# Inverse blocks in four parts, key products by chunks, and two first tiles prepared a stage ahead

## The reference

```
q, k, v = [silu(causal_conv4(x @ W.T)) for W in (Wq, Wk, Wv)]
beta = sigmoid(x @ Wb.T)
q, k = l2norm(q), l2norm(k)
# per head and per chunk of 32 tokens
A = strict_lower(-(beta*k) @ k.T);  T = inverse(eye - A)
u = T @ (beta*v);  w = T @ (beta*k)
# scan over chunks with state S
u_adj = u_i - w_i @ S
o_i = q_i @ S + causal(q_i @ k_i.T) @ u_adj;  S = S + k_i.T @ u_adj
# three causal per-channel filters of v, 3, 15 and 63 taps, and a gate
probs = softmax((x @ gate_w + gate_b) / exp(log_temp)) * (1 - 5*eps) + eps
o = p0*fir_s(v) + p1*fir_m(v) + p2*fir_l(v) + p3*delta + p4*v
attn = rmsnorm(o) @ Wo.T
x1 = layernorm(x + attn);  out = layernorm(x1 + ffn(x1))
```

## Time and profile before

| | us |
|---|---|
| median of 3 runs | 2274.93 |
| lowest, highest | 2270.86, 2278.68 |
| the profiled execution itself | 2272.73 |
| its span, first to last instruction | 2270.9 |
| TensorE busy in the span | 2067.6 (91%) |
| VectorE, ScalarE, GpSimd busy | 1163.6, 884.8, 521.0 |

### The profile page before, as it was taken

How to read it: one execution, slowest core, us unless ns; L and a number is a source line. 1 busy time by engine, 2 the same in 40 slices (tenths; PEclk the granted TensorE clock), 3 DMA queues, 4 the chain that set the end, 5 groups by cost and what they waited for, 6 DMA issues and landing times.

```text
span 2270.9 us, 41455 instructions
## 1 busy us (share of the span) xinstructions
PE 2067.6 (91%) x16936; PEld 1753.8 (77%) x16936; DVE 1163.6 (51%) x1803; ACT 884.8 (39%) x1438; POOL 521.0 (23%) x530
## 2 busy tenths in 40 slices
PE   7888882778699999599999999999999999999998
PEld 5776762667588887488888888888888888888886
DVE  5777776974377776334334434434433443443442
ACT  4455541110244444234434434434443443443442
POOL 1111777875355555100000000000000000000000
PEclk9999995798699999699999999999999999999999
DMA  5666667677999996100000000000000000000000
GB/s 166 195 195 167 209 181 195 222 220 276 211 233 236 238 236 161 60 1 28 1 28 28 1 28 28 1 28 28 6 23 28 29 1 28 28 1 28 28 1 19
DMA packets 246751, 217.02 MB, mean 96 GB/s; under 512 B 158786, under 2 KB 210498, under 8 KB 241986
## 3 DMA queue, kind: packets, MB, share of 16 engines
q1 hardware_dynamic: 234306, 184.29, 29.6%
q10 hardware_dynamic: 12288, 30.41, 4.5%
HBM read 130.52 MB, written 84.15 MB: 95 GB/s over the span
## 4 chain that ended last, share of the span: by engine, by line
PE 56%; DVE 1%; issue 1%; ACT 1%; DMA 0%; POOLq 0%; DVEq 0%; SPq 0%; POOL 0%; ACTq 0%
PE B L1534 50%; PE O L1561 5%; PE T L1492 1%; DVE yb L1667 0%; ACT gate L1606 0%; DMA srow<-in_srow 0%; DVE stats L1695 0%; DVE stats L1729 0%; ACT L1606 0%; DVE x L1690 0%; DVE z L1720 0%; DVE xl L1647 0%; DVE z L1724 0%; DVE x L1708 0%; DVE z L1743 0%
## 5 line engine op out<-in xcount | busy, mean ns | idle before, releaser
L1620 ACT ACTIVATE yb<-B,scol 128x512 f32<-128x512 f32 x256 | 176.7, 690 | 580.2 <-PE B L1534 580.2
L1534 PE MATMUL B<-act1l,wr 128*128 128x512 f32 x1024 | 398.5, 389 | 0.0
L1534 PE MATMUL B<-act0h,wr 128*128 128x512 f32 x1024 | 398.3, 389 | 0.0
L1534 PE MATMUL B<-act0l,wr 128*128 128x512 f32 x1024 | 398.3, 389 | 0.0
L1534 PE MATMUL B<-act1h,wr 128*128 128x512 f32 x1024 | 398.3, 389 | 0.0
L1655 DVE TENSOR_TENSOR act0l<-yb,act0h 128x512 fp32r<-128x512 f32 x256 | 176.2, 688 | 317.4 <-ACT act0h L1623 315.2
L453 DVE SCALAR_TENSOR_TENSOR acc<-proj,taps,acc 128x512 f32<-128x512 f32 x288 | 214.7, 750 | 84.4 <-ACT acc L399 75.8
L1655 DVE TENSOR_TENSOR act1l<-yb,act1h 128x512 fp32r<-128x512 f32 x128 | 88.6, 692 | 295.5 <-ACT act1h L1623 295.5
L1534 PEld LDWEIGHTS B<-act0l,wr 128*128 128x128 f32 x1024 | 192.2, 188 | 39.9
L1534 PEld LDWEIGHTS B<-act1l,wr 128*128 128x128 f32 x1024 | 192.2, 188 | 39.9
L1534 PEld LDWEIGHTS B<-act1h,wr 128*128 128x128 f32 x1024 | 192.2, 188 | 39.9
(11 more groups left out here) (169 smaller groups left out, 3204.0 us busy)
## 6 DMA issues: line engine op xcount, KB each, us to landing
qk_s<-yT SPq DMA_DIRECT2D x16, 1024.0 KB, 6.1
kk_s<-kfull SPq DMA_DIRECT2D x16, 1024.0 KB, 6.4
qk<-qk_s SPq DMA_DIRECT2D x32, 512.0 KB, 4.2
wraw<-in_ffn_w ACTq DMA_DIRECT2D x32, 352.0 KB, 5.0
toe<-in_toe_short ACTq DMA_DIRECT2D x32, 320.0 KB, 7.4
xt<-in_xt SPq DMA_DIRECT2D x16, 524.0 KB, 4.3
k_s<-ktok SPq DMA_DIRECT2D x16, 512.0 KB, 7.2
v_s<-vtok SPq DMA_DIRECT2D x16, 512.0 KB, 3.2
```

Of the source, the lines that this page charges most:

```text
L1534: last = nc.tensor.matmul(B[slot % 4][:, :], w, part, start=(k == 0 and i == 0), stop=(k == kts - 1 and i == len(parts) - 1))
L1620: last = nc.scalar.activation(dst, B[slot % 4][:, :], ACT.Gelu, scale=scol[:, slot:slot + 1])
```

## The change

The inverse's 8 slots are cut into four parts of 2 slots and 4 steps each. Parts 0 and 1 go to GpSimd within project, parts 2 and 3 to VectorE in weights_fir, where their 60 operations lie in groups 4 to 55 instead of 0 to 29. Key products are made per 64 tokens, all in `keys`, with 64 x 64 results; `kk_s` is half as large. The steps of project are written out without loops. Gate tables of three quarters of the rows are computed in project after steps 4, 8 and 12; weights_fir computes the last quarter. Window 0 of `win` is filled by SP from `vtok` in project, the first three Toeplitz tiles are loaded at its start. The load and norm of the first feed-forward tile stand at the end of delta. `y` has two buffers. In the diff, `gate_logits` stands for four operations of VectorE (bias, temperature, maximum, subtraction), `gate_shares` for five (sum, reciprocal, slope, scaling, eps). The pieces are, in order: constants and `blocks_in`, SP, TensorE, ScalarE and VectorE in project, VectorE in weights_fir, SP and VectorE in delta, and the size of `kk_s`.

```diff
+EARLY = 2
+EARLY_COLS = {6: (0, 1, 8), 7: (0, 8, 14), 8: (0, 14, 20), 9: (0, 20, 31),
+              10: (1, 1, 8), 11: (1, 8, 14), 12: (1, 14, 20), 13: (1, 20, 27), 14: (1, 27, 31)}
...
+        first = q // 2 * PGRP + t * NS % PGRP
+        queue.dma_start(keep["tri"][first:first + NS, c * PSLOTS + q % 2, :, :],
...
+                    sp.dma_start(win0[:, NT + t * BATCH:NT + (t + 1) * BATCH, :], vtok[p][:, 0, :, :]).then_inc(v_stored[p], 16)
+                    sp.dma_start(win0[WIN:P, t * BATCH:(t + 1) * BATCH, :], vtok[p][0:WIN, 0, :, :]).then_inc(v_stored[p], 16)
+                    if t + 1 < STEPS:
+                        sp.dma_start(win0[0:WIN, (t + 1) * BATCH:(t + 2) * BATCH, :], vtok[p][WIN:P, 0, :, :]).then_inc(v_stored[p], 16)
...
+                    for s in range(BH):
                         b, hh = s // KT, s % KT
+                        for chunk in HALVES:
+                            for par in range(2):
+                                kt = yT[p][64 * par:64 * par + DK, KT + hh, b * P + chunk.start:b * P + chunk.stop]
+                                last = nc.tensor.matmul(side[par][chunk, s * HC:s * HC + HC], kt, kt, start=True, stop=True)
+                    last.then_inc(kk_ready, 1)
...
-                after = {0: keys, 1: lambda t, p: squared(t, p, 2), 2: small, 4: values}
+                after = {0: keys, 2: small, 4: values}
...
+                for t in range(STEPS):
+                    step(t, t % 2, t // 2, t > 0)
...
+                for n in range(NTOE):
+                    toeplitz(act, io, keep, n)
+                act.wait_ge(prm_in, 16)
+                nc.scalar.activation(itemp[:, :], prm[:, NGATE:NGATE + HEADS], ACT.Exp, scale=-1.0).then_inc(itemp_done, 1)
...
+                for t in range(1, STEPS):
+                    step(t, t % 2, (t - 1) // 2, True, t < 2)
+                    if t % PART_STEPS == 0:
+                        c = t // PART_STEPS - 1
+                        act.wait_ge(small_out, t + 1)
+                        if c < EARLY:
+                            if c:
+                                act.wait_ge(gam0_done, c)
+                            nc.scalar.activation(ebeta[:, :, :], raw[:, c * NE:c * NE + NE, NGATE:NGATE + HEADS], ACT.Exp,
+                                                 scale=-1.0).then_inc(exp0_done, 1)
+                        act.wait_ge(to_exp0, c + 1)
+                        nc.scalar.activation(lg0[:, :, :, :], lg0[:, :, :, :], ACT.Exp).then_inc(exp0_done, 1)
...
+                for t in range(1, STEPS):
+                    step(t, t % 2, (t - 1) // 2, True)
+                    if t % PART_STEPS == 0:
+                        first_logits(t // PART_STEPS - 1)
+                        if t // PART_STEPS <= EARLY:
+                            first_scales(t // PART_STEPS - 1)
+                    if t % PART_STEPS == 1 and t > 1:
+                        first_shares(t // PART_STEPS - 1)
...
+def gate_logits(nc, link, keep, lg, mx, rows):
...
+def gate_shares(nc, link, keep, lg, mx, rows):
...
+        OPS = 2 * (CH - 2)
+        SUB_FIRST, SUB_END = 4, 4 + OPS * 13 // 15
+        D_OUT, T_OUT = {2: 0, 6: 1, 29: 2, 30: 3}, {4: 0, 8: 1, 30: 2, 31: 3}
+        TURNS = {2: (0,), 5: (1,), 28: (2, 3)}
...
+                    if n == 1:
+                        for c in range(EARLY, PARTS):
+                            blocks_there(dve, keep, c)
+                        dve.wait_ge(tables_out, 3)
+                        dve.wait_ge(above_zero, 1)
+                        sub.scaled_columns().then_inc(columns_scaled, 1)
+                        dve.wait_ge(columns_scaled, 1)
+                    if n == 2:
+                        query_scales()
+                    if SUB_FIRST <= n < SUB_END:
+                        for i in range((n - SUB_FIRST) * 15 // 13, (n - SUB_FIRST + 1) * 15 // 13):
+                            link(sub.update(i // 2 + 1) if i % 2 else sub.outer_product(i // 2 + 1))
+                    if n == SUB_END:
                         dve.wait_ge(upper_zero, 1)
+                        sub.scaled_rows().then_inc(keep["inv_done"][1], 1)
...
+                for p in range(2):
+                    sp.wait_ge(y_stored[p], 48)
+                sp.dma_start(keep["x1"][:, :, :], row(io["y_s"], 0)).then_inc(keep["x1_in"][0], 16)
+                sp.dma_start(keep["xres"][:, :, :], io["x"][:, 0:P, :].rearrange("b p d -> p b d")).then_inc(keep["xres_in"], 16)
...
+                nc.vector.tensor_tensor(x1[:, :, :], x1[:, :, :], xres[:, :, :], ALU.add).then_inc(keep["x1_sum"], 1)
...
-    "kk_s": (P, GRP, P),
+    "kk_s": (P, GRP, HC),
```

More of the change, by code:

```diff
@@ new lines, in toeplitz, with by_matrix @@
+def toeplitz(act, io, keep, n):
+    toe, toe_in = keep["toe"][n % NTOE], keep["toe_in"][n % NTOE]
+    act.dma_start(toe[:, NF - 1, :, :], io["toe_long"][n]).then_inc(toe_in, 16)
+    act.dma_start(toe[SHORT:, 0:NF - 1, :, :], io["toe_short"][n]).then_inc(toe_in, 16)
+def by_matrix(nc, gam, half):
+    for par in range(2):
+        last = nc.vector.tensor_copy(gam[:, :, par, :],
+                                     half.rearrange("p (v b) (k r) -> p v r (b k)", b=GB, r=2)[:, :, par, :])
+    return last
@@ L560, in weights_fir, with turn_scales @@
+def turn_scales(nc, out, gam, ident, parts=1):
+    for c in range(parts):
+        for rows in HALVES:
+            last = nc.tensor.matmul(out[rows, c * HC:c * HC + HC],
+                                    gam[rows, c * 2 * PART_STEPS:(c + 1) * 2 * PART_STEPS, :, :].rearrange("p t r s -> p (t r s)"),
+                                    ident[rows, rows], start=True, stop=True)
+    return last
 def weights_fir(nc, sems, io, keep):
@@ L726, in _, with turn @@
[L726 to L729 removed]
+                def turn(c):
+                    inverses_there(act, c)
+                    if c >= 2:
+                        act.wait_ge(turned_stored[c % 2], 64 * (c // 2))
+                    nc.scalar.activation(turned_inv[c % 2][:, :, :, :],
+                                         tri[:, c * PSLOTS:c * PSLOTS + PSLOTS, :, :].rearrange("p q i c -> p q c i"),
+                                         ACT.Copy).then_inc(turned, 1)
@@ L744, in _ @@
                 for n in range(HEADS * DK // TCH - NTOE):
                     act.wait_ge(conv_ready, (n + 1) * PER_TOE)
-                    toeplitz(n + NTOE)
-                    if n in TURNS:
-                        turn(TURNS[n])
+                    toeplitz(act, io, keep, n + NTOE)
+                    for c in TURNS.get(n, ()):
+                        turn(c)
             @block.vector
@@ L1382, in ffn @@
         ln_eps = outer.sb("ln_eps5", [P, BATCH])
-        x1 = [outer.sb(f"x1{i}", [P, BATCH, D]) for i in range(2)]
+        x1 = [keep["x1"], outer.sb("x11", [P, BATCH, D])]
         z = [outer.sb(f"z{i}", [P, BATCH, D]) for i in range(2)]
```

459 lines of the change are left out of this document (221 added, 238 removed).

## The result

The changed kernel took 2243.6 us (median of 4 runs, 2240.09 to 2253.28) against 2276.8 (4 runs on the same chip): a ratio of 0.9868, interval 0.9839 to 0.9897. It is about 30 us (1.3%) faster, where 47 to 49 were forecast. The time lies in the range 2207 to 2247, 18 us above the point, and outside the 2215 to 2238 that the forecast claimed for itself. The profiled execution took 2240.09 us with a span of 2238.3, 32.6 less than before.

The account below looks back on a forecast made before the run. Bounds: a TensorE-ScalarE-VectorE ring in projections, VectorE then TensorE in the filter loop, TensorE in the feed-forward. Projections -4, filter stage -34.6, entry -8.7: -47.3 us, forecast 2226 (chance 0.50), own range 2215 to 2238, wide range 2207 to 2247.

Parts of the forecast that it names:

- Gate tables and scales three times inside: Projections: three places of gate and scale work cost 12 us against 5 for one before: +7 us (0 to +15).
- The filter stage: Second stage, weights_fir: preamble -24.9, loop -12.7 and its end +3 us, together -34.6 us.
- Rival A: Filter loop: transfers set its time, 196 us at 226 GB/s; stage gains 21 us, not 34.6; 2240 in all; chance 0.15.
- C: Filter preamble goes only in part, tables still wait for slow clock or a transfer: 16 us more, 2242; chance 0.08.
- Key products by chunks: Projection steps: TensorE's 1.33 us wait goes, 0.65 us a step gained: -9.8 us (0 to -20); last step -2.8.
- the ends of the loops' 0.3: Projections: unrolling saves the odd 0.3 us at each loop turn, six iterations: -1.7 us (0 to -12).
- Start, stage end, ninth step, preamble: Projections: start +3 us, end -1.5, GpSimd overrun in the ninth step +1.5; filter preamble, first weighting at 9 us: -24.9.
- The loop: Filter and inverse loop: 151 us plus 10 for transfers and low clock, 161 against 173.7: -12.7 us (-22 to -4).
- the charge of GpSimd: Filter loop: GpSimd's operations delay VectorE's inverse work by 0.42 us in each of 52 groups.
- the reading that the prediction set aside: Filter loop: the 0.42 us paid per pair of operations, 30 times as before; the loop would be 9 us less.
- below 5 us: Filter loop: sign that TensorE's waits for toe, the filter tiles, stay under this total.
- Stage end and entry of the feed-forward: Filter stage's end: late block stores, +3 us (0 to +8); feed-forward entry without the tile's loads: -8.7 us (-7 to -9.5).

Follow-up runs that it names:

- e_warm2: Changed kernel plus unread TensorE matmuls in the two steps behind each gate place, cut to the gap (7 and 3, then 6): 2231.9 us, ratio 0.9812.
- e_warm: Changed kernel plus unread TensorE matmuls in the two steps behind each gate place (12 and 5, then 11): 2239.0 us, ratio 0.9833.
- e_dense: Changed kernel with VectorE's inverse operations at the old density, two a group in groups 4 to 33: 2255.4 us, ratio 0.9909.
- e_place: Changed kernel with gate and scale pieces behind steps' last filters and exponentials in ScalarE's gap before a step's last SiLU: 2234.6 us, ratio 0.9825.

## Why the prediction was right in direction and too large

**The step that failed** is the term "Gate tables and scales three times inside": 12 us for three places against 5 for the one before, +7. The places cost 31.7 us, less 1.1 that the step after the second regains: about +26. (GpSimd was 1.1 us late to one square; TensorE's steps show the same sum.) The price of the work itself was set somewhat low: at a clock of 1.00 it is 3.6 us at the first place (e_warm2; forecast 2.7), at most 7.8 at the second (e_warm; 5.2), 6.2 at the third (e_warm2). The prediction had 4.2 for that one. Together at most 17.6 for 12, so of the 19 us that the term is off, at most 6 are the work and the rest, 13 or more, is a term that the prediction did not have: TensorE's lower clock behind its wait. It is 6.8 of 10.4 us at the first place and 3.4 of 9.6 at the third. The prediction read the clock in the loop and never in the projections. The hint was there: the earlier trace rows gave one place at 23.31, and it was taken as the price of the work, while the clock was down in that very step of the kernel before:

```profile
215.00:220.00 5.00, 3.71 (x21) 3.08 (x22) 2.25 (x3) 3.21 (x7) 0.00 (x0) 0.66 1.01 230
```

**The total is nearer than its parts.** The filter stage won 39.2 us where 34.6 were forecast, which covers a quarter of the miss in the projections. 2243.6 lies where rivals A (2240) and C (2242) stood, and neither happened: the preamble went whole, and the filter stage gained more and not less. That the time is inside the wide range is in part luck.

**Key products by chunks.** Quiet steps of 19.6 us: met, with the ends of the loops' 0.3. The step had a second effect, not forecast: two waits of TensorE became one of 1.7 us. That this made the falls of the clock likelier is argued, not shown.

**Start, stage end, ninth step, preamble.** First xt at 13.2 us and not 9.1; the stage's last stretch 27.8 us (31.0 before); GpSimd had no gap in front of the square after step 9 and was 1.1 us late to it, which VectorE did not feel (1.5 us were booked for it); first weighting 9.4 us into the stage (9 forecast). All met within 1.5 us, though 1.9 of the 24.9 us forecast for the preamble were a wait of the second weighting, which stands in the loop of the table (it took 1.92 us).

**The loop.** -17.5 where -12.7 was forecast. Too high was the charge of GpSimd: the groups on VectorE are now

```profile
L155 DVE TENSOR_TENSOR outer<-tri 128x120 f32<-128x120 f32 (+14 forms) x30 | 32.6, 1086 | 0.1
L159 DVE TENSOR_TENSOR tri<-tri,outer 128x120 f32<-128x120 f32 (+14 forms) x30 | 32.1, 1069 | 0.1
```

64.7 us, against 63.1 in the earlier trace rows and 72.2 forecast (50.4 bare and 0.42 for each of 52 groups). The price goes by the operations, 30 pairs times 0.48 (in e_dense, two to a group, 63.1 us), not by groups: the reading that the prediction set aside, worth 7.5 us. And the waits for tiles, called "below 5 us", came to more than the 8.7 us before, not less:

```profile
PE conv L781 <- DMA toe<-in_toe_short: 16.4, 8, 2.8
PE conv L781 <- DVE prods L875: 13.2, 13, 2.1
```

So of the forecast 151 + 10 us the first was 7.5 too high and the second some 3 too low (1.9 of them the wait just named), which makes 156. Rival A had its share of truth: at a DMA share of 0.86 TensorE waits 16.4 of 156 us for tiles. But the transfers ran at 258 GB/s where it reckoned with 226.

**Stage end and entry of the feed-forward.** +4.7 for +3, from the blocks stored last: no engine works from 538.83 to 550.36 at 297 GB/s. The entry's chain ran as described in the earlier trace rows, without the tile's loads:

```profile
911.16 4.69 DMA srow<-in_srow
...
919.64 5.37 PE B L1622 x13
```

## What to carry to other kernels

Where TensorE waits in every step, an insertion on another engine can cost more than its length, by the clock behind the longer wait: 10.4 us here for 3.6 of work. Read the granted clock behind each wait, not only the mean of the stage. Put small VectorE work where VectorE waits and GpSimd is quiet, and fill what gap TensorE keeps with matmuls that nobody reads, shorter than the gap. In a loop where two engines and the transfers take turns, spread side work evenly: it was worth 20 of 176 us here.

## What was not expected of the hardware

- The granted clock fell to 0.5 behind waits of 1.96, 2.58 and 3.92 us between bursts of TensorE, and stayed there for some 3 to 12 us of full work; behind 1.97 and 2.50 us in the same kernel (e_place) it held. The same place, unchanged, was at 0.50 for 5 us and more in one kernel and at a mean of 0.83 in another. The Trainium skill, TensorE: Matmul & The Clock Gate, section Why this matters for your kernels, warns of gaps between matmul bursts, but of longer ones than the first two here; by it steps 5 and 10 of e_place would have kept their clock. The measurement decides.
- A VectorE product of 128x64 in SBUF took 0.23 us alone and 1.80 beside a GpSimd square; `tensor_scalar` 0.19 and 1.08; reductions and reciprocals were not touched (0.49 and 0.55 in both).
- Identical delta-rule code took 357.4 to 369.3 us from kernel to kernel, at a granted 0.94 and 0.93.
